# Squaring each layer's weights in one ScalarE operation, and adding one column of sums on TensorE in place of two

## The reference

```
xn = layernorm(x)
g, v, d = xn @ Wg + bg, xn @ Wv + bv, xn @ Wd + bd
a       = 0.001 + 0.998 * sigmoid(d)
scan[t] = a[t] * scan[t-1] + sigmoid(g[t]) * tanh(v[t])        # along each sequence

scores  = sigmoid(xn @ Wg2.T + bg2 + bias)                     # 8 experts
weights = the two highest scores of each token, 0 elsewhere
expert_e(xn) = gelu(xn @ W1[e].T + b1[e]) @ W2[e].T + b2[e]    # 256 -> 1024 -> 256
shared(xn)   = gelu(xn @ Ws1.T + bs1) @ Ws2.T + bs2

out = x + scan + shared(xn) + sum_e weights[:, e] * expert_e(xn)
```

## Time and profile before

| | |
|---|---|
| median of 3 runs | 690.43 us (690.24 to 690.6) |
| profiled execution | 689.23 us, of which the span of the trace is 687.4 |
| busy share of the span | PE 96%, PEld 76%, DVE 75%, ACT 63%, POOL 42% |
| TensorE's granted clock | 0.997 of full speed |

### The profile page before, as it was taken

One profiled execution on the slowest core, in us unless ns is written; L12 is line 12 of the kernel. 1 busy time (PEld: TensorE's weight loads), 2 busy tenths in 40 slices (PEclk: granted clock), 3 DMA queues, 4 the chain that ended last, 5 costly groups with the idle time before them and its releaser, 6 DMA issues.

```text
span 687.4 us, 20158 instructions
## 1 busy us (share of the span) xinstructions
PE 660.7 (96%) x5872; PEld 521.4 (76%) x5873; DVE 512.9 (75%) x1334; ACT 433.6 (63%) x738; POOL 288.0 (42%) x261
## 2 busy tenths in 40 slices
PE   5899999999999998899999999999999999999995
PEld 4465757566666756788889888888889888898774
DVE  5899899999899889776666666666666666666653
ACT  6988696969696865455555555555555555554652
POOL 3133332414242634244546455454645445463512
PEclk9999999999999999999999999999999999999998
DMA  7534335252524231233334243333424333342412
GB/s 255 185 76 141 99 118 138 82 180 61 182 60 154 62 123 33 63 55 62 57 60 67 54 69 52 63 57 59 66 54 69 51 64 56 60 69 48 78 33 32
DMA packets 54173, 57.56 MB, mean 84 GB/s; under 512 B 13204, under 2 KB 48916, under 8 KB 54136
## 3 DMA queue, kind: packets, MB, share of 16 engines
q1 hardware_dynamic: 38456, 38.42, 18.8%
q0 software_dynamic: 15680, 18.69, 17.1%
HBM read 38.53 MB, written 18.55 MB: 83 GB/s over the span
## 4 chain that ended last, share of the span: by engine, by line
PE 84%; DVE 6%; issue 4%; DMA 2%; ACT 2%; POOLq 0%; SPq 0%; POOL 0%; DVEq 0%; ACTq 0%
PE bank L1239 34%; PE bank L1231 33%; PE bank L1219 7%; PE bank L1258 3%; PE bank L1288 2%; PE bank L1270 2%; DVE arena L897 1%; PE bank L1175 1%; DVE W L801 1%; PE bank L1210 1%; DMA arena<-in_gates 1%; DVE arena L898 1%; PE bank L1192 1%; PE bank L1184 1%; DVE arena L840 1%
## 5 line engine op out<-in xcount | busy, mean ns | idle before, releaser
L1239 PE MATMUL bank<-W,arena 128*128 (+1 forms) x2304 | 303.0, 273 | 4.0 <-DVE arena L898 4.0
L1231 PE MATMUL bank<-rows,W 128*128 128x256 f16 (+1 forms) x1920 | 298.5, 294 | 2.3 <-ACT arena L593 1.2
L1239 PEld LDWEIGHTS bank<-W,arena 128*128 128x128 f16 x2304 | 222.4, 98 | 41.9 <-DVE arena L898 4.0
L1231 PEld LDWEIGHTS bank<-rows,W 128*128 (+1 forms) x1920 | 185.8, 98 | 56.2 <-issue 2.9
L593 ACT ACTIVATE arena<-bank,par 128x256 f32<-128x256 f32 x256 | 137.0, 561 | 77.4 <-PE bank L1231 57.7
L506 POOL DMA_INDIRECT out<-arena,slot_add x64 | 109.7, 1714 | 150.9 <-ACT arena L730 141.2
L897 DVE TENSOR_SCALAR arena<-arena,par 128x256 f16<-128x256 f32 x284 | 101.4, 357 | 62.0 <-ACT arena L593 41.4
L898 DVE SCALAR_TENSOR_TENSOR arena<-arena,par 128x256 f16<-128x256 f32 x284 | 139.0, 489 | 10.0
L442 POOL DMA_INDIRECT lists<-entry,place x64 | 71.7, 1121 | 122.8 <-ACT arena L579 67.0
L491 POOL DMA_INDIRECT rows<-xhl_rows,slot_list x64 | 69.4, 1085 | 40.4 <-DMA slot_list<-lists 23.1
L601 ACT ACTIVATE rows<-bank 128x1024 f16<-128x1024 f16 x32 | 32.8, 1024 | 57.1 <-PE bank L1288 57.1
(11 more groups left out here) (162 smaller groups left out, 520.7 us busy)
## 6 DMA issues: line engine op xcount, KB each, us to landing
stage<-in_w SPq DMA_DIRECT2D x32, 512.0 KB, 4.8
b2row<-in_b SPq DMA_DIRECT2D x39, 128.0 KB, 2.9
arena<-in_x SPq DMA_DIRECT2D x8, 512.0 KB, 5.1
xhl_rows<-W SPq DMA_DIRECT2D x8, 512.0 KB, 4.6
out<-arena SPq DMA_DIRECT2D x8, 512.0 KB, 5.4
W<-in_w SPq DMA_DIRECT2D x4, 512.0 KB, 9.4
lists<-entry,place POOLq DMA_INDIRECT x64, 3.3
rows<-xhl_rows,slot_list POOLq DMA_INDIRECT x64, 2.8
```

What stands on the lines that cost most here:

```text
L1231: ins = T.matmul(bank_, weights(w, wp * HALF + c * H + j * P, P), rhs[:, 2 * xp + c, :], start=n == 0, stop=n == 3 * KD - 1)
L1239: ins = T.matmul(banks[t // 2][:, (t % 2) * D:(t % 2 + 1) * D], h[:, hp, t * P:(t + 1) * P], weights(w, (2 + wp) * HALF + j * D, D), start ...
```

## The change

Sets 2 to 8 (the third to the ninth), which are prepared in sequences 1 to 7, are squared a layer at a time: one ACTIVATE over 2048 columns in place of two over 1024, with one column of `ssq` for its sum. Layer 0 is squared behind `score` alone, where it had its second half; layer 1 behind gelu 1 alone. Sets 0 and 1 keep their halves. PE's `norm_sum` of sets 2 to 8 leaves out the second matmul, as the odd columns of `ssq` hold nothing for these sets.

```diff
+            def layer_squares(n, l):
+
+                for part in range(2):
+                    act.wait_ge(w_in[l][part], n * 16)
+                if l == 0:
+                    act.wait_ge(norm_ok, n + 1)
+                o = n * WSET + l * 2 * HALF
+                if isinstance(n, int) and n == NW - 1:
+
+                    o = at + 4 * SEQ if l == 0 else n * WSET
+                ins = A(W[:, bass.ds(o, HALF)], landing(n, l), ACT.Square, accum_out=ssq[:, 2 * l:2 * l + 1])
+                if l == 1:
+                    ins.then_inc(ssq_ok, 1)
...
@@ sequence(b, u, last_) on ACT
-                    if i == 1:
-                        squares(b + 1, 0, 0)
                     if i == 4:
                         score(b)
-                        squares(b + 1, 0, 1)
+                        layer_squares(b + 1, 0)
...
                     gelu_wide(b, u, i)
-                    if i in ((1, 2) if last_ else (0, 1)):
-                        squares(b + 1, 1, i - last_)
+                    if i == 1:
+                        layer_squares(b + 1, 1)
...
@@ norm_sum(n, sums) on PE
-                for part in range(2):
-                    ins = T.matmul(sums, onesf[:, :], halves[:, :, part], start=part == 0, stop=part == 1)
+                parts = 2 if isinstance(n, int) and n < 2 else 1
+                for part in range(parts):
+                    ins = T.matmul(sums, onesf[:, :], halves[:, :, part], start=part == 0, stop=part == parts - 1)
```

## The result

| | before | after |
|---|---|---|
| median of 14 runs each | 689.98 us (689.3 to 690.6) | 691.59 us (690.59 to 692.15) |
| ratio after to before | | 1.0023, 95% interval 1.0016 to 1.0030 |
| span of the profiled execution | 687.4 | 689.3 |
| PE, DVE, ACT busy, us | 660.7, 512.9, 433.6 | 660.8, 514.9, 431.2 |

The change costs 1.6 us (689.98 to 691.59). ACT has 2.4 us less to do and the kernel is slower. The forecast was +0.6 us, with +1.8 for the rival in which the wide square delays more.

What follows compares the result with a forecast made beforehand. A loop through PE and DVE was taken to set the pace in sequences 2 to 5. PE's matmuls 0, sequences 2 to 5 +0.49, sequences 1 and 6 +0.1: +0.6 us on 690.43, so 691.0; range 689.7 to 692.1.

Steps and rivals of the forecast that it cites:

- the rival in which the wide square delays more: Square takes 2.08 us or semaphores hold it up by 0.2; split 0 later, +1.8 us, 692.2; chance 0.12.
- the likeliest case: Split 0 slightly late behind layer 0's wide square: +0.6 us, 691.0, own range 690.6 to 691.6; chance 0.58.
- a loss of over 0.2%: Slower by more than 1.4 us: most of the delaying rival and a little of the forecast; chance 0.13.
- PE's matmuls are worth nothing: Two of four norm_sum rows go, 0.19 us a sequence, but PE then waits for DVE's split: gain 0.
- The 0 for sequences 1 and 6: PE's saved norm_sum time was taken to gain 0 in sequences 1 to 6, these two included.
- The square costs 1.88 us: On ACT, a whole layer's square takes 1.88 us against 2.08 for two halves; bounds 1.69 and 2.08.
- 4.11 us from the square to split 0: Square, projection 5, decay, gelu 0, then DVE's split: split 0 late by 0.07 to 0.85 us in sequences 1 to 6.
- In sequences 2 to 5 everything from split 0 to the residual is DVE's own work in a row, so the lateness reaches PE whole: Split 0's lateness reaches PE at the transposes behind block 2: 0.07 + 3 x 0.14 = 0.49 us.
- Sequences 1, 6 and 7 cost 0.1: Sequences 1 and 6 lose 0.05 to 0.1 us together; in 7 projection 5's scan wait covers the wider square.
- The rule on breaking up operations: Where ACT isn't saturated but holds up others, smaller instructions finish work sooner; it speaks against merging squares before projection 5.

Runs made afterwards that it cites:

- the kernel with the sum alone: Kernel before with only PE's second norm_sum matmul left out for sets 2 to 8, squares still in halves: 689.75 us, ratio 1.0002.
- With the collision taken away: Changed kernel, with POOL's last scatter of the sequence before also waiting for DVE's place and entry tables in sequences 1 to 6: 689.91 us, ratio 1.0008 against before.

## Why the prediction was right, and where it fell short

The time lies in the range, the direction of the likeliest case was right, its size was not: +0.6 us forecast, +1.6 measured. That 691.59 lies within the likeliest case's own 690.6 to 691.6 is luck, as before measured 0.45 us lower in these runs than in the three that the forecast started from. And a loss of over 0.2% had a chance of just 0.13; the measured 0.23%, with an interval of 0.16 to 0.30, stands about on that line.

*PE's matmuls are worth nothing.* Right for the time. They were 0.23 us a sequence rather than 0.19, and the kernel with the sum alone measured 1.0002. The 0 for sequences 1 and 6 isn't quite right: that kernel's trace gained 0.2 in each. In the changed kernel the late split took it: sequence 6 has the 31.75 us of before.

*The square costs 1.88 us.* Right: 1.89 from its start to the next instruction. The rival that needed a square of 2.08 us came near the measured time, but by a mechanism that wasn't there.

*4.11 us from the square to split 0.* Right in sequences 1 and 6, where split 0 came 0.84 and 0.29 us later against the transposes of the sequence before, forecast 0.85 and 0.30. In sequences 2 to 5 it is a tenth more: in sequence 3 it was 128.03 - 123.83 = 4.20. The last piece, gelu 0 to the split, is 128.03 - 127.14 = 0.89 us there and not the 0.79 that I had from sequence 1; why is open. (Gelu 0, which the prediction puts at 127.05, is at 127.02 by its own terms; nothing rests on it.) Counted from the transposes of sequence 2 (105.12 us before, 105.24 after), split 0 came 0.24 us later than before, where the forecast was 0.14.

*"In sequences 2 to 5 everything from split 0 to the residual is DVE's own work in a row, so the lateness reaches PE whole."* This is the step that fell short, for it took the duration of DVE's work as fixed. The lateness did reach PE whole, but it also moved two small rows into the later part of POOL's scatter issue, and they grew by 0.2 us together with what is behind them. The sum per sequence was 32.27 - 31.86 = 0.41 us: 0.22 to 0.24 for the lateness and 4.92 - 4.73 = 0.19 for the collision. Over sequences 3 to 5 that is 1.2 us where I had 0.4, and sequence 2 adds 0.25 where I had 0.07. With the collision taken away the measured cost was 0.6 us, the forecast's number; some of that agreement is chance, as the lateness was a tenth larger in each of these sequences and the interval is 1.2 us wide.

*Sequences 1, 6 and 7 cost 0.1.* About right, it was nothing. In the two traces the spacing of the transposes from sequence 5 to 6 is 31.75 us in both, sequence 1 took 33.31 after and 33.37 before, and projection 4 of sequence 7 is 251.93 against 250.53, 1.4 us late. The rest of the 1.9 us between the two spans lies behind it, in transfers (the last scatter to SP's next row took 0.5 longer), and is of the size by which single executions differ.

*The rule on breaking up operations* (the Trainium skill, Perfetto Trace Analysis, Optimizing Scalar/DVE Operations) held in this case: the merged square in front of projection 5 gave ACT less to do and the other engines a later start, 1.0023. Layer 1's merged square, which nothing waits for, cost nothing and gained nothing (1.0001). For layer 0 no place was found that gains, and behind projections 1 and 2 the kernels measured from 1.0003 to 1.0020, for the reasons above and in part for none that is known.

## What to carry to other kernels

When two operations are merged, one of them moves: price the merged one at its new place in the queue, from there to the engine that sets the pace, and not by the engine's total. A path that has been just long enough hands every tenth of a microsecond on, once per round of the loop. And a row's duration holds for what runs beside it now: when a change shifts an engine against another, look at what its rows will then stand next to, above all small DVE rows and POOL's issue of indirect DMAs. And where one operation waits for two loads, it needs the second one as early as the first; ask when that lands in other executions too, and not only in the one profiled. The last round of a loop can want another order than the others, because other work hangs on it.

## What the runs showed of the hardware

DVE operations with one input were lengthened by POOL's issue of an indirect DMA, but only late in it. With the cast at 0.28 us behind the start of a 1.03 us issue, it and the 8-column operation behind it took 0.17 us each; with the cast at 0.64 us behind it, 0.38 and 0.31. The kernel before shows it too, once: in sequence 1 the cast at 0.55 us behind the issue's start took 0.17, the operation at 0.63 took 0.38. In the kernel with the square behind projection 1 it was split 2's first operation, while POOL issued from 133.19 to 134.18 (DVE's timeline, sequence 3; 0.49 in the kernel before):

```profile
133.66 0.74 DVE L910 TENSOR_SCALAR arena<-arena,PT 128x512 f16<-128x512 f32 x1
```

In the changed kernel it was also split 3's first operation, behind the residual, while POOL issued from 136.82 to 137.77; before it took 0.48:

```profile
137.38 0.61 DVE L909 TENSOR_SCALAR arena<-arena,PT 128x512 f16<-128x512 f32 x1
```

These rows started 0.47 to 0.71 us behind an issue's start and all ended at a set distance from its end: those with 8 columns about 0.02 us ahead of it, those with 512 columns 0.22 behind it. That looks as if DVE was held until the issue ended, which is inferred from these rows. The scan, an operation with two inputs, wasn't lengthened: in the kernel before it started 0.50 us behind the issue's start, ran past its end and took 1.22 us, the same as in the changed kernel, where it started when the issue had ended.
